# A routed feed-forward kernel on one core: later weight chunks split during the first stage, base products all ahead of the first gather

## The reference, cut to what matters

```python
x = x + tanh(g_xattn[0]) * xattn(layernorm(x), fside, ctx)      # quantised, per batch
x = x + tanh(g_ffn[0]) * ffn(layernorm(x), ...)
# ffn:
conf = sigmoid(x @ conf_W.T + conf_b); bids = conf * expert_wealth
top_bids, sel = top_k(bids, 2); routing = softmax(top_bids)
base_g = x @ base_gate; base_u = x @ base_up                    # 256 -> 896 each
for e in range(8):
    g = base_g + x @ gate_A[e] @ gate_B[e] * 0.25               # rank 64
    u = base_u + x @ up_A[e] @ up_B[e] * 0.25
    h = silu(g) * u
    oe = h @ base_down + h @ down_A[e] @ down_B[e] * 0.25
    out = out + sum(routing * (sel == e)) * oe
```

## Time and profile before

| | |
|---|---|
| median of 3 runs | 347.58 us (346.81 to 350.02) |
| the profiled execution's own time | 349.11 us |
| its span, first to last instruction | 347.20 us |
| mean granted clock of TensorE | 0.875 of 2.4 GHz |
| PE busy / DVE / ACT / POOL | 261.5 / 201.3 / 167.1 / 133.8 us |

### The profile page before, as it was taken

The page is one execution under the profiler, slowest core; times in us unless marked ns, Lnnn a source line. Parts: engine busy times, 40 slices in busy tenths (PEclk is TensorE's granted clock), DMA queues, the critical chain, the costliest instruction groups (busy, mean ns, idle before and its releaser), DMA issues.

```text
span 347.2 us, 5197 instructions
## 1 busy us (share of the span) xinstructions
PE 261.5 (75%) x1540; PEld 236.1 (68%) x1541; DVE 201.3 (58%) x409; ACT 167.1 (48%) x285; POOL 133.8 (39%) x162
## 2 busy tenths in 40 slices
PE   2569547988981003995999999999999999997700
PEld 1446435877971002994999999999999999996600
DVE  4598997661497000016667767777777677776115
ACT  2448875756354351253555545555555555555011
POOL 5396614220057995018233333333333333311111
PEclk9855997899996555898999999999999999999755
DMA  8545210025348674226244444444444444400065
GB/s 255 166 124 124 62 31 30 32 106 206 161 154 248 189 206 127 105 120 217 83 135 146 139 130 137 142 138 139 143 141 135 144 137 138 145 21 15 17 205 173
DMA packets 30190, 45.69 MB, mean 132 GB/s; under 512 B 13976, under 2 KB 25632, under 8 KB 30176
## 3 DMA queue, kind: packets, MB, share of 16 engines
q0 software_dynamic: 4416, 21.50, 18.7%
q1 hardware_dynamic: 21840, 14.55, 14.8%
q10 hardware_dynamic: 3920, 9.46, 7.2%
HBM read 33.57 MB, written 11.93 MB: 131 GB/s over the span
## 4 chain that ended last, share of the span: by engine, by line
PE 62%; DVE 10%; DMA 10%; POOL 6%; ACT 6%; issue 3%; SPq 2%; ACTq 0%; DVEq 0%
PE pY L55 8%; PE pY L59 7%; PE pY L57 7%; PE pG L55 5%; PE pT L1548 4%; PE pG L57 4%; PE pG L59 4%; PE pU L57 3%; PE pU L59 3%; PE pU L55 3%; DMA q<-in_ctx_dram 3%; PE bank L1254 2%; DMA yr<-results 2%; DMA raw<-in_L_ffn_down_A_dram 2%; POOL WdA_lo L440 2%
## 5 line engine op out<-in xcount | busy, mean ns | idle before, releaser
L525 POOL DMA_INDIRECT results<-yb,dest x19 | 18.8, 987 | 94.4 <-DVE yb L1188 94.4
L55 PE MATMUL pY<-Wd_hi,hT_hi 128*128 128x384 f32 x133 | 48.3, 363 | 1.1 <-ACT Wd_lo L789 0.8
L59 PE MATMUL pY<-Wd_hi,hT_lo 128*128 128x384 f32 x133 | 45.3, 341 | 0.0
L57 PE MATMUL pY<-Wd_lo,hT_hi 128*128 128x384 f32 x133 | 45.3, 341 | 0.0
L519 POOL DMA_INDIRECT bin<-base_products,tok x18 | 22.0, 1220 | 26.9 <-PE pU L59 17.1
L799 ACT CAST hT_hi<-pT 128x896 fp32r<-128x896 f32 x19 | 17.2, 907 | 24.1 <-PE pT L1548 24.1
L1511 PE MATMUL pX<-ident,xin 128*128 128x128 f32 x38 | 7.5, 280 | 27.9 <-DMA xin<-normed,tok 27.9
L55 PEld LDWEIGHTS pY<-Wd_hi,hT_hi 128*128 128x128 f32 x133 | 25.4, 191 | 3.3 <-issue 1.0
L775 ACT CAST xaT_hi<-pX 128x256 fp32r<-128x256 f32 x19 | 7.1, 374 | 42.5 <-PE pX L1525 42.1
L1118 DVE TENSOR_TENSOR xT_lo<-pX,xT_hi 128x256 fp32r<-128x256 f32 x19 | 7.9, 416 | 31.0 <-ACT xT_hi L769 31.0
L57 PEld LDWEIGHTS pY<-Wd_lo,hT_hi 128*128 128x128 f32 x133 | 25.6, 193 | 0.0
(11 more groups left out here) (234 smaller groups left out, 778.4 us busy)
## 6 DMA issues: line engine op xcount, KB each, us to landing
base_products<-brow ACTq DMA_DIRECT2D x8, 896.0 KB, 3.6
yr<-results SPq DMA_DIRECT2D x8, 256.0 KB, 5.4
raw<-in_L_ffn_down_A_dram SPq DMA_DIRECT2D x7, 256.0 KB, 3.0
raw<-in_L_ffn_gate_B_dram SPq DMA_DIRECT2D x8, 224.0 KB, 2.8
raw<-in_L_ffn_up_B_dram SPq DMA_DIRECT2D x8, 224.0 KB, 2.8
x_resid<-in_x_dram SPq DMA_DIRECT2D x4, 256.0 KB, 5.1
q<-in_fside_BxS2xS_dram ACTq DMA_DIRECT2D x4, 256.0 KB, 5.7
normed<-q ACTq DMA_DIRECT2D x4, 256.0 KB, 2.2
```

The source lines that it names most:

```text
L55: m.matmul(outs[i], hi, whi[i], start=first, stop=False, skip_group_check=True)
L57: m.matmul(outs[i], hi, wlo[i], start=False, stop=False, skip_group_check=True)
L59: ins = m.matmul(outs[i], lo, whi[i], start=False, stop=last, skip_group_check=True)
L525: g.indirect_dma_start(out=yg, out_offset=bass.IndirectOffsetOnAxis(ap=dest[:, j:j + 1], axis=0), in_=yb[:, :], in_offset=None).then_inc(d ...
```

## The change

- The ring of raw chunks has six slots instead of four.
- ScalarE casts twelve of the 25 later chunks between the steps of stage one, up to base_store(1), and the rest between its last evacuations of base products.
- POOL makes twelve low parts between roots2, gated and deviations2 of stage one, the other 13 behind deviations2(3).
- TensorE makes all base products ahead of the first gathered rows: the order is base_half(3, ·), the rank products, base 4, base 5, half (6, 0), the sorted products, half (6, 1), base 7. Before, half (4, 0) stood ahead of the rank products, the sorted products behind base 5, and base 6 and 7 behind x_T(0). ScalarE evacuates base 6 and 7 before it waits for the plan.
- Behind x_T(0) come project_A(0), the direct gate products, xa_T(0), and the direct up products (`direct`).

```diff
-        RING, RW = 4, 512
+        RING, RW = 6, 512
...
@@ POOL
             lo(1)
             roots2(1)
+            lo(4)
             gated(2)
             deviations2(0)
+            lo(1)
             roots2(2)
+            lo(1)
             gated(3)
             deviations2(1)
+            lo(1)
             roots2(3)
+            lo(4)
             deviations2(2)
+            lo(1)
             deviations2(3)
             lo(CH_1 - lo_done[0])
...
@@ ACT
             integers_w(2)
-            split(1)
+            split(3)
             scaled2(0)
             scales_w(2)
             integers2(0)
+            split(1)
             scales_c(0)
+            split(1)
             weights_scaled(3)
...
             normal2(0)
+            split(1)
             scales_w(3)
             x2_hi(0)
+            split(1)
             silu1(3)
+            split(2)
             conf_rows(0)
...
             integers2(2)
+            split(1)
             scaled2(3)
...
             integers2(3)
+            split(1)
             base_half(1, 0)
             scales_c(3)
+            split(1)
             normal2(2)
             base_half(1, 1)
             base_store(1)
+            split(1)
             x2_hi(2)
...
             conf_rows(3)
+            split(1)
             act.wait_ge(s_logit, 1)
             a.activation(bids[:, :, :], bids[:, :, :], ACT.Sigmoid).then_inc(s_sig, 1)
+            split(2)
             base_half(3, 0)
+            split(1)
             base_half(3, 1)
             base_store(3)
+            split(2)
             base_half(4, 0)
...
+            split(2)
             base_half(4, 1)
             base_store(4)
             split(2)
...
             base_store(5)
-            split(2)
             split(CH_1)
-
+            for t in range(PRE, NT):
+                base_out(t)
...
             x_hi(0)
-            for t in range(PRE, NT):
-                base_out(t)
             xa_hi(0, first=True)
...
@@ PE
             base_half(3, 1)
-            base_half(4, 0)
...
             ins.then_inc(s_rank, 1)
-            base_half(4, 1)
-            base_half(5, 0)
-            base_half(5, 1)
+            base(4)
+            base(5)
+            base_half(6, 0)
...
             ins.then_inc(s_sorted, 1)
+            base_half(6, 1)
+            base(7)
...
+            def direct(gu):
+
+                pe.wait_ge((s_bgc, s_buc)[gu], NT)
+                for c in range(HC):
+                    ins = base_product((pG, pU)[gu], gu, c, xT_hi[:, c, :], xT_lo[:, c, :], False)
+                return ins
+
             x_T(0)
-            base(PRE)
             pe.wait_ge(s_wlo, CH_A)
             project_A(0, group(0))
-            base(PRE + 1)
+            direct(0)
             xa_T(0)
-
-            for gu, copied in enumerate((s_bgc, s_buc)):
-                pe.wait_ge(copied, NT)
-                for c in range(HC):
-                    ins = base_product((pG, pU)[gu], gu, c, xT_hi[:, c, :], xT_lo[:, c, :], False)
-            ins.then_inc(s_direct, 1)
+            direct(1).then_inc(s_direct, 1)
             pe.wait_ge(s_xalo, 1)
             x_T(1)
```

## The result

| | before | predicted | after |
|---|---|---|---|
| median | 347.20 us (346.81 to 350.02, 4 runs) | 326.7 (317 to 335) | 324.89 us (323.24 to 325.88, 4 runs) |
| the profiled execution: time, span | 349.11, 347.20 | 328.2 | 324.35, 322.4 |
| its mean granted clock | 0.875 | | 0.944 |

Measured side by side, after takes 0.9336 of the time of before (95% interval 0.9271 to 0.9402); by the medians it is 22.3 us less.

What follows compares the result with a forecast made beforehand. POOL's 25 low parts delayed the first gather and left TensorE idle 27.88 us. Second transposes move from 154.46 to 133.6, stage one and routing costs included: 20.9 us saved, so 326.7 us, range 317 to 335.

Steps and rivals of the forecast that it cites:

- The hole: TensorE ahead of the first xin transposes: 27.9 us of idle falls under 2; second transposes 8.0 us behind the first.
- First stage, POOL's order: POOL, stage one: low parts 11 and 12, waiting for casts, stand ahead of deviations2(2) and deviations2(3); +3.6 us.
- First stage, casts and holds: Stage one: one cast on ScalarE's chain, +0.6 us; some three VectorE operations held by low parts, +3.1 us.
- Routing: Transposes of the logits to rank products: five low parts hold VectorE, pickb comes 10.5 us behind; +2.5 us.
- Behind the rank products: VectorE from the rank products to the plan: 16.4 us, left unchanged; plan at 120.3.
- The ring: Ring of six chunk slots: priced at nothing beyond the hole's waits; 3.2 us kept as bound of its cost.
- A: Stage one: the low parts hide there at no cost; 314.5 to 320 us; chance 0.2.
- B: Stage one: every low part holds VectorE's chain, 11.0 us in place of 3.1; 334.6 us; chance 0.14.
- C: TensorE stays at the 1.2 GHz level from 58 to 134; slower than before, 361 us; chance 0.02.
- D: POOL's queue: chunks land late, the 13 last low parts again end after the plan; 327 to 338 us; chance 0.04.

Runs made afterwards that it cites:

- splits_only: The changed kernel with base 6 and 7 back behind the first gather, casts, low parts and ring as changed; 334.2 us.
- base_only: The kernel before, with its ring of four and its splits, and only the base products moved ahead of the gather; 343.56 us.
- dev_first: The changed kernel with low parts 10 and 11, ahead of deviations2(2), and 12 moved behind deviations2(3); 321.23 us.
- dev_hold: dev_first with POOL's later low parts held until VectorE has written pickb; 326.44 us.
- hold_pickb: The changed kernel with POOL's last 13 low parts held until VectorE has written pickb; 328.59 us.
- dev_shift_early: dev_shift with two casts around the sigmoid moved up to scales_c(3) and normal2(2); 321.16 us over 7 runs, ratio 0.923.
- dev_shift: dev_first with the low parts ahead of roots2(2) and roots2(3) moved behind them; 321.54 us over 6 runs.
- no_stage: The changed kernel without the twelve casts and low parts in stage one; all 25 low parts follow deviations2(3); 331.63 us.
- base_only_ring6: base_only with a ring of six slots in place of four; 337.84 us.
- before_ring6: The kernel before with a ring of six slots and nothing else changed; 343.64 us.

## Why the prediction was right, and where its terms were off

The sum by its own steps, all from the profiled executions; what was measured is counted in the view in order of time, which has the second x_T of before at 154.30:

| step | predicted | measured |
|---|---|---|
| first stage, to the transposes of the logits | +7.3 (86.01 to 93.3) | +5.6 (91.64) |
| from there to the rank products | +2.5 (8.04 to 10.5) | -0.6 (7.47) |
| rank products to the first x_T | -20.4 (42.17 to 21.8) | -19.9 (22.31) |
| first to second x_T | -10.2 (18.24 to 8.0) | -10.2 (18.08 to 7.88) |
| second x_T to the end of the span | 0 (192.7) | +0.2 (192.9 to 193.1) |
| sum | -20.9 | -24.8 |

**The hole** (right). It closed as written: the last lo ends at 114.58 (foretold 118), ahead of the plan, the four halves of base 6 and 7 at full clock fill the rest, and the second transposes come 7.88 behind the first (8.0). splits_only and base_only show that it takes both halves of the change. That it came out at full clock is in part luck, since four other kernels without the hole (`dev_first`, `dev_hold`, `hold_pickb`, `dev_shift_early`) had 0.82 or 0.83 there, and TensorE was busy 1.4 to 1.5 us longer for the same products. Which came last at x_T(0) was wrong by a little: TensorE was free at 120.75 and the gather landed 0.67 later. I had the gather 1.8 earlier than TensorE. I issued it 0.1 behind the end of tok; it was issued 1.0 behind it (116.37 to 117.41), since POOL waits for share, the next operation, too, and took 0.9 more. And I let the rows land after 3.4 us, as in the hole; they took 4.0, beside loads and stores.

**First stage, POOL's order** (right). I had +3.6 for the path to the last logits; dev_first shows 2.7 by its marks and 3.1 counted from roots2(3). The two casts stood behind the steps that I had named (76.59 and 82.49), and each deviations2 waited for the cast as well as for its lo: 1.9 and 3.9 us by dev_first (76.42 and 80.34 against 78.36 and 84.24).

**First stage, casts and holds** (the size nearly right, the places only partly). I had 0.6 + 3.1 = 3.7. What dev_first, without the order's share, still has against base_only's 85.03 is 3.9. The rows show held operations at 57.33 and 63.12, beside lo 5 and lo 7 as I had walked them, and four more at 46.87, 49.16, 69.16 and 77.71, with 0.6 to 1.1 us each. The first two lie on the path: dev_shift got back 0.96 and 0.57 us for them. Up to roots2(3) casts and holds together cost some 3 us (21.49 from roots2(1), 18.30 to 18.58 in the five kernels without these lo's); how the other 1.5 divide is not shown.

The measured +5.6 looks better than it is. Kernels whose first stage is that of before, but whose clock was full from 20 to 36, have their transposes at 85.03 (base_only), 84.61 (no_stage), 84.44 (base_only_ring6) and 83.99 (before_ring6), not 86.01. Against these the first stage costs 6.6 to 7.7, and 7.3 stands between. Of the 24.8 in the table 0.9 is the clock of one execution (last section), and up to 1 more is what this stage differs between kernels that are the same there or differ only in the ring; by medians 22.3 were saved against 20.9 foretold.

**Routing** (the step that failed, in an outcome inside the range). I wrote: "five lo's (13 to 17) now run beside its two rounds of maxima", "Five hits of 1.13 make 5.6, pickb comes at 10.5". Four ran there, since POOL waited 6.60, 0.78 and 1.87 us for casts that stand between evacuations, and the fifth fell behind pickb. And a hit costs not the length of a lo but the part of it that is left when the operation comes: 0.25, 0.75, 0.85 and 0.65 over the free 0.22, 2.5 in all. pickb came 7.4 behind the transposes, TensorE waited 1.72 and not 5, and with the half (4, 0) gone from ahead of the rank products the step ended at -0.6.

**Behind the rank products** (nearly right). I left the 16.4 us to the plan as they were; they were 17.3 (99.11 to the end of tok at 116.37), with a new hold on csum, 1.07 us.

**The ring** (mis-sized, harmlessly). "I price it at nothing more" holds within 2 us by the medians (3.4 by the ratios) for the whole change, but the ring alone is worth 3.1 on before and 5.7 with the base products ahead. The waits for landings, which I took as part of the hole, set the hole's length.

**Rivals.** A fell: the first stage was not free. B fell too: 11.0 us were never near, operations out of PSUM passed. C fell: the granted clock was 1.00 from 91.6 to the mark. D fell: the 13 lo's were out 1.8 before the plan. In after the clock was below full in stretches only, not as one long state: 0.67 and 0.71 from 48 to 64.5, 0.79 from 80 to 88, and behind the mark 0.63 from 137 to 145 and the end.

## What to carry to other kernels

Fill a hole with work that needs nothing of what is awaited, and shorten it from the other side at the same time: each alone left 6.8 and 19.8 us of idle, the pair 0.7. Work that is put on a waiting engine goes behind the short step that others wait for, never ahead of it, above all where it waits for a third engine itself; two lines moved gave 3.7 us more. And a conflict between two engines is not removed by holding one back: the work comes out in one block beside the next chain, where it costs more.

## What the runs showed of the hardware

**One held operation per low part.** In hold_pickb, with POOL's lo's (1.1 us each) back to back, VectorE's small operations took 1.08, 2 x 1.09 and 1.08 us where 0.16 to 0.18 is their length: one operation to one lo. What passes freely is as plain: line 1094, which has one input in PSUM (0.22 at 103.27), and the reductions (line 1097, 0.22). It goes the other way too: in no_stage two lo's took 4.48 us beside VectorE's long operations, 2.5 elsewhere. By the Trainium skill, "SBUF — State Buffer", section "SBUF: two separate sides", the shared port pair is locked for a whole instruction by whichever engine comes first; the trace agrees, in both directions.

**The clock differs between executions of the same work.** The first stage is the same up to 36 us in nearly all these kernels. Before, then before_ring6:

```profile
20.00:36.00 16.00, 12.56 (x55) 9.88 (x55) 14.09 (x32) 12.11 (x24) 10.94 (x15) 0.52 0.43 101
```

```profile
20.00:36.00 16.00, 10.20 (x62) 7.85 (x60) 14.90 (x35) 12.37 (x25) 11.39 (x15) 1.00 0.45 103
```

Two of the thirteen profiles (before and splits_only) have the 1.2 GHz level there. What it costs can be read between two of POOL's operations that all thirteen have, the one on q at 33.91 of before (L472) and the power at 38.91 (L476): 5.00 and 5.01 us in these two, 4.10 to 4.11 in the other eleven. So these two are 0.9 us late from then on. A single profile is therefore no measure of 1 us in such a stage. Distances between two marks close to each other, set side by side over all kernels that share the stretch, are a better one: they made the roots of dev_shift readable, which its medians did not.
